# An adaLN transformer block: which round of the attention loop computes the projections of the next head pair

## The chip, the cores and the metric

The kernel runs on one core of one Trainium2 chip. The metric is device time in microseconds (us) from launch to end. Five engines run their own instruction streams and wait for each other through semaphores: PE (TensorE, matmuls), ACT (ScalarE), DVE (VectorE), POOL (GpSimd) and SP (SyncE, which here only issues DMAs). A matmul writes PSUM, which has eight banks of 128 x 512 f32; ACT and DVE read it from there.

## What is computed

Two adaLN blocks over four batches of 1024 tokens with 256 channels. The change touches only the first block's causal attention with 16 heads of 64, and the modulation vectors that are worked out beside it in the first batch:

```python
mod = (silu(L0_c) @ L0_wmod).reshape(4, 6, 1, -1)      # and the same for block 1
h = layernorm(x) * (1 + ca) + sa
latent_kv = h @ w_kv_down
k, v = split(latent_kv @ w_kv_up)                      # 16 heads of 64
q = h @ w_q
att = softmax(where(causal, q @ k.T * 64 ** -0.5, -inf))
x = x + ga * ((att @ v) @ w_out)
```

After it come a low-rank FFN, a second block with linear attention and MLP, and a mixture of experts; none of that is changed.

## The kernel before

Batch after batch goes through all stages. In the attention of a batch the heads go in `PAIRS` = 8 pairs, and each pair in three rounds (`ROUND_TILES` = (0, 2, 1, 5), (3, 7), (4, 6)): a round takes query tiles of 128 rows whose causal parts add up to 12 blocks of 128 keys, so each round has the same matmul work in scores and in values. There are `ROUNDS` = 24 rounds. Round m is the first of its pair when m is a multiple of 3; "a third round" is one with m = 2, 5, 8 and so on.

One round goes through the engines like this:

- PE `scores(m)` (L666) fills the score banks. It may start once DVE has taken the minima of round m-1.
- DVE `minimum` (L794) adds the mask, keeps the masked scores in SBUF and takes row minima, one call for a tile and a head. ACT `exponential` (L917) follows each. Once the last of a head is there, DVE `shuffle` (L801) transposes 32 x 32 blocks. After a third round come the reciprocals of the row sums, and `store_inverse` and `spread_inverse` send them through DRAM into `inverse_wide`.
- POOL `keep` (L865, seven copies) and SP `MOVES` (L1007, nine DMAs) bring the shuffled blocks into `placed`.
- PE `values(m)` (L688) multiplies `placed` by `v_t`. It stands two rounds later in PE's stream, behind `scores(m + 2)`. ACT `read_values` (L925) copies the result from `out_bank` into `yT`, and POOL `norm` (L875) scales it, four rounds after.

The projections of a pair are six jobs, `JOBS` = q0, q1, k0, k1, v0, v1, halves of the query, key and value projections (PE L710, L714, L720; ACT copies L901, L903, L905). `round_of` says in which round a pair's jobs stand. From round 2 on all jobs write one bank, `job_bank`, so each must wait until ACT has copied the one before. The first job of a round stands ahead of `values(m - 2)` on PE, the second behind it; `jobs_ahead` names the first. On ACT the copy of the first stands among the last exponentials of the round, that of the second behind `read_values`.

Into the first batch's rounds the modulation is fitted. `mod_products` (round 1), `mod_columns`, `mod_take` and `mod_values` (round 2) work it out. `mod_turn` (PE L756) transposes it into `out_bank`, `mod_rows_copy` (ACT L947) copies it out, and the next `values` may write `out_bank` only after that.

In the last rounds there are no jobs left. `output_part` (PE L730) starts the output projection of tiles 0 and 1 from the pairs that are scaled already, as filler, and behind the loop `head_output` (L1134) does the same for other tiles. The first work that needs the last pair is L1118: it waits for `norm` of round 21, and that for the last spread of the reciprocals.

Engines run their streams in the order in which the code is written; nothing is reordered by a scheduler. Before the change:

```python
def round_of(pair, j):
    return ROUNDS_OF * (pair - 1) + (JOBS.index(j) // 2 if (pair, j) != (1, "v0") else 1)
```

So pair 3, for one, had q0 and q1 in round 6, k0 and k1 in round 7, v0 and v1 in round 8. PE's stream of a round was:

```python
scores(m)
ahead = jobs_of(m) if m < FILLING else jobs_ahead(m)
for j in ahead:
    job(*j)
if m > 1:
    values(m - 2)
for j in jobs_of(m)[len(ahead):]:
    job(*j)
```

## Time and profile before

| | us |
|---|---|
| median of 3 runs | 1703.29 |
| the runs | 1703.29, 1702.17, 1703.40 |
| profiled execution, own time | 1701.55 |
| its span | 1700.1 |
| PE busy in the span | 1655.3 |
| DVE busy | 1225.7 |
| POOL busy | 868.3 |
| ACT busy | 846.6 |

The times of the rows are from the start of the span. The profiled execution is 1.74 us under the median of the three runs, and 1.45 us of it lie outside the span. The attention rounds of the four batches begin near 25, 450, 868 and 1285 us, and each takes about 205 us.

### The profile page before, as it was taken

To read this page: it belongs to the slowest core of one execution; us is meant where nothing else is said; L and a number is where in the kernel's file an instruction comes from. 1 tells how busy PE (TensorE), PEld (TensorE's weight loads), DVE (VectorE), ACT (ScalarE), POOL (GpSimd) and SP (SyncE) were. 2 spreads that over 40 slices of the span, in tenths; PEclk is the share of its full clock that TensorE was granted. 3 is DMA by queue.
4 is the path that set the end of the run, shared out by engine and by line. 5 is a ranking of instruction groups with operands and counts; after the bars stand their busy time and mean duration, and the time that the engine had idled before them with its cause. 6 is when DMAs were issued, how large, how long until landed. Compare 5 with 4: busy or idle time off the path is not lost.

```text
span 1700.1 us, 41069 instructions
## 1 busy us (share of the span) xinstructions
PE 1655.3 (97%) x16550; PEld 1133.1 (67%) x16550; DVE 1225.7 (72%) x2674; ACT 846.6 (50%) x1872; POOL 868.3 (51%) x1127
## 2 busy tenths in 40 slices
PE   9999999999999999999999999999999999999997
PEld 5566685768566667576856667756784666766666
DVE  5898957636699994762779997675468999677445
ACT  5667634233577762422457775432246776443232
POOL 3788853142188884222228888324114888731420
PEclk9999999999999999999999999999999999999999
DMA  6466572141565665032356655405045666620504
GB/s 193 121 157 152 140 180 94 29 72 44 160 153 137 151 144 170 1 63 38 89 136 157 149 144 135 149 2 96 5 118 133 148 152 144 157 106 2 100 0 126
DMA packets 143853, 189.11 MB, mean 111 GB/s; under 512 B 34512, under 2 KB 107696, under 8 KB 142640
## 3 DMA queue, kind: packets, MB, share of 16 engines
q1 hardware_dynamic: 125472, 179.14, 43.0%
q10 hardware_dynamic: 18192, 7.35, 1.8%
q8 instruction: 131, 2.15, 0.6%
q14 instruction: 58, 0.48, 0.1%
HBM read 88.32 MB, written 13.16 MB: 60 GB/s over the span
## 4 chain that ended last, share of the span: by engine, by line
PE 76%; DVE 13%; ACT 5%; POOL 2%; issue 2%; DMA 1%; SPq 1%; ACTq 0%; DVEq 0%; POOLq 0%
PE scores L470 13%; PE scores L666 11%; PE bank L688 11%; PE bank L470 5%; PE bank L710 4%; PE bank L714 3%; ACT prob L917 3%; PE bank L720 2%; DVE prob L801 2%; PE scores L1785 2%; PE scores L1725 2%; DVE hx L801 2%; PE scores L441 2%; PE scores L1134 2%; ACT hx L917 1%
## 5 line engine op out<-in xcount | busy, mean ns | idle before, releaser
L865 POOL COPY placed<-prob 32x768 f32<-32x768 f32 x448 | 368.0, 821 | 207.6 <-DVE prob L801 165.6
L301 POOL TENSOR_TENSOR rstd<-rstd,minus_half 128x2 f32<-128x2 f32 (+1 forms) x100 | 71.9, 721 | 486.7 <-DVE rstd L300 484.6
L688 PEld LDWEIGHTS bank<-placed,v_t 128*64 128x64 f32 x4608 | 255.0, 137 | 39.6 <-issue 39.4
L666 PE MATMUL scores<-k_t,q_t 64*128 64x512 f32 (+3 forms) x1536 | 274.0, 496 | 3.0 <-DVE neg_max L794 3.0
L688 PE MATMUL bank<-placed,v_t 128*64 128x128 f32 x4608 | 269.4, 273 | 1.9 <-DMA placed<-prob 1.7
L801 DVE STREAM_TRANSPOSE prob<-prob 128x1536 f32<-128x1536 f32 x128 | 220.0, 1757 | 37.0 <-ACT prob L917 37.0
L794 DVE CUSTOM_DVE_ANT_0 mod_rows<-scores,hx 128x128 f32<-128x128 f32 (+7 forms) x256 | 190.9, 746 | 37.6 <-PE scores L666 37.2
L666 PEld LDWEIGHTS scores<-k_t,q_t 64*128 64x128 f32 x1536 | 130.4, 187 | 116.6 <-issue 95.0
L865 POOL COPY placed<-hx 32x768 f32<-32x768 f32 x224 | 184.1, 822 | 30.5 <-DVE hx L801 13.5
L917 ACT ACTIVATE prob<-mod_rows,neg_max 128x128 f32<-128x128 f32 (+2 forms) x192 | 137.3, 715 | 118.8 <-DVE neg_max L794 115.9
L794 DVE CUSTOM_DVE_ANT_0 x<-scores,hx 128x128 f32<-128x128 f32 (+7 forms) x256 | 192.7, 753 | 0.0
L917 ACT ACTIVATE prob<-x,neg_max 128x128 f32<-128x128 f32 (+2 forms) x192 | 136.2, 709 | 0.0
L801 DVE STREAM_TRANSPOSE hx<-hx 128x1536 f32<-128x1536 f32 x64 | 112.0, 1750 | 6.2 <-ACT hx L917 6.2
L710 PE MATMUL bank<-hT,w_ring 128*64 128x512 f32 x448 | 108.2, 607 | 2.8 <-ACT q_t L901 2.8
L875 POOL TENSOR_TENSOR yT<-yT,inverse_wide 128x256 f32<-128x256 f32 (+2 forms) x128 | 91.7, 730 | 26.4 <-DMA inverse_wide<-inverse_scratch 19.4
L917 ACT ACTIVATE hx<-mod_rows,neg_max 128x640 f32<-128x640 f32 x64 | 59.9, 936 | 75.1 <-DVE neg_max L794 75.1
L1062 DVE TENSOR_TENSOR tmp<-bank,mod_rows 128x256 f32<-128x256 f32 x28 | 11.8, 423 | 115.0 <-PE bank L1118 70.0
L470 PE MATMUL scores<-mT,w 128*128 128x512 f32 x192 | 85.0, 592 | 0.0
L720 PEld LDWEIGHTS bank<-w_ring,latT 128*64 128x64 f32 x1024 | 55.1, 136 | 30.3 <-issue 18.2
L925 ACT COPY yT<-bank 128x256 f32<-128x256 f32 (+2 forms) x128 | 43.1, 362 | 60.5 <-PE bank L688 60.4
L720 PE MATMUL bank<-w_ring,latT 128*64 128x128 f32 x1024 | 68.6, 277 | 2.7 <-ACT k_t L903 2.7
L710 PEld LDWEIGHTS bank<-hT,w_ring 128*64 128x64 f32 x448 | 28.9, 137 | 59.5 <-issue 56.1
(253 smaller groups left out, 3107.3 us busy)
## 6 DMA issues: line engine op xcount, KB each, us to landing
placed<-prob SPq DMA_DIRECT2D x576, 96.0 KB, 2.6
f<-in_L_ffn_f SPq DMA_DIRECT2D x16, 2048.0 KB, 13.8
placed<-hx SPq DMA_DIRECT2D x288, 96.0 KB, 2.2
inverse_wide<-inverse_scratch SPq DMA_DIRECT2D x64, 256.0 KB, 4.3
slots_scratch<-high_rows SPq DMA_DIRECT2D x16, 512.0 KB, 6.6
inter<-slots_scratch SPq DMA_DIRECT2D x32, 256.0 KB, 4.7
mod_rows<-mod_scratch SPq DMA_DIRECT2D x32, 128.0 KB, 4.8
out<-x SPq DMA_DIRECT2D x16, 256.0 KB, 2.1
```

The costliest lines, as they stand in the source:

```text
L301: step = pool.do(lambda e, ts=ts: nc.gpsimd.tensor_tensor(rstd[:, ts], rstd[:, ts], minus_half[:, ts], op=ALU.pow), var, filled)
L470: step = pe.do(lambda e, n=n, w=w, m=m: nc.tensor.matmul(ps, w, m, start=n == 0, stop=n == len(pieces) - 1), copy, *after)
L666: last = nc.tensor.matmul(score_tiles[head][:, at_ // 512, at_ % 512:at_ % 512 + hi - lo], q_t[buf][rows_, tile * P:(tile + 1) * P], k_t[b ...
L688: last = nc.tensor.matmul(out_bank[rows_, at_:at_ + P], v_t[pair % 2][:, j, rows_], placed[m % 2][:, :, head, first_block(m, i) + j, :], s ...
L710: last = nc.tensor.matmul(ps[side, :], ring[:, c * P + side.start:c * P + side.stop], hT[:, c, cols], start=c == 0, stop=c == C - 1)
L714: last = nc.tensor.matmul(ps[side, :], ring[:, 2 * P + side.start:2 * P + side.stop], latT[:, cols], start=True, stop=True)
L720: last = nc.tensor.matmul(ps[side, t * P:(t + 1) * P], latT[:, at_ + side.start:at_ + side.stop], ring[:, 3 * P:4 * P], start=True, stop=True)
L794: nc.vector.tensor_tensor_reduce(masked_scores[head][:, cols], score_tiles[head][:, :, :].rearrange("p a n -> p (a n)")[:, cols], future[: ...
L801: nc.vector.transpose(p_, p_).then_inc(flow["shuffled"], 1)
L865: nc.gpsimd.tensor_copy(placed[m % 2][target * GROUP:(target + 1) * GROUP, source, :, :, :], prob[m % 3][source * GROUP:(source + 1) * GRO ...
L875: last = nc.gpsimd.tensor_tensor(dst, dst, out_place(m, lo, hi, inverse_wide), op=ALU.mult)
L917: nc.scalar.activation(prob[m % 3][:, :, head, blocks_in(m, i), :], masked_scores[head][:, columns_in(m, i)].rearrange("p (n g i) -> p g n ...
```

## The change

From the third pair on (`pair` 2 and up, counted from 0) every job moves by one place: q0 goes one round earlier, behind its `values`; q1 and k0 share the next round, then k1 and v0, then v1 with q0 of the following pair. The places themselves, one ahead of `values` and one behind, stay. In the first batch's round 2 both jobs stand behind `values(0)`. ACT copies the first job of round 3 (first batch) or of round 2 (other batches) ahead of all exponentials of that round. `mod_turn` and `mod_rows_copy` go from the end of round 3 into round 4: the turn behind `scores(4)`, the copy behind the first two exponentials. `output_part(0)` goes from round 22 to round 21.

```diff
         def jobs_of(m):
             pair = m // ROUNDS_OF + 1
-            return [(pair, j) for j in JOBS if round_of(pair, j) == m] if pair < PAIRS else []
+            return [(p, j) for p in (pair, pair + 1) if p < PAIRS for j in JOBS if round_of(p, j) == m]
 
         def round_of(pair, j):
-            return ROUNDS_OF * (pair - 1) + (JOBS.index(j) // 2 if (pair, j) != (1, "v0") else 1)
+            if pair < 2:
+                return ROUNDS_OF * (pair - 1) + (JOBS.index(j) // 2 if (pair, j) != (1, "v0") else 1)
+            return ROUNDS_OF * (pair - 1) + (JOBS.index(j) - 1) // 2
...
-        MOD_ROUND = 3
+        MOD_ROUND = 4
...
-                if b == 0 and m == MOD_ROUND - 1:
+                if b == 0 and m == MOD_ROUND - 2:
                     e.wait_ge(flow["mod_rows_ready"], 1)
...
             def mod_turn():
-                e.wait_ge(flow["values_read"], MOD_ROUND - 1)
+                e.wait_ge(flow["values_read"], MOD_ROUND - 2)
...
+                if b == 0 and m == MOD_ROUND:
+                    mod_turn()
                 ahead = jobs_of(m) if m < FILLING else jobs_ahead(m)
                 for j in ahead:
                     job(*j)
+                if m == ROUNDS - 3:
+                    output_part(0)
                 if m == ROUNDS - 1:
                     output_part(1)
-                if m == ROUNDS - 2:
-                    output_part(0)
                 if m > 1:
                     values(m - 2)
                 for j in jobs_of(m)[len(ahead):]:
                     job(*j)
-                if b == 0 and m == MOD_ROUND:
-                    mod_turn()
...
+                if m == 2 and b or m == 3 and b == 0:
+                    for j in ahead:
+                        job(*j)
                 for i in range(large):
                     for head in range(HEADS):
                         exponential(m, i, head)
+                    if b == 0 and i == 0 and m == MOD_ROUND:
+                        mod_rows_copy()
...
                 early = m == 1 or len(tiles_in(m)) > 2
+                if m == 2 or m == 3 and b == 0:
+                    early = None
                 for j in ahead if early else ():
                     job(*j)
                 exponential(m, large, 0)
-                for j in ahead if not early else ():
+                for j in ahead if early is False else ():
                     job(*j)
...
-                if b == 0 and m == MOD_ROUND:
-                    mod_rows_copy()
```

PE's stream in the first batch, from `values(0)` in round 2 to `scores(4)`, before (L688 values, L720 v1 of pair 1, L666 scores, L710 q jobs, L756 the modulation's turn):

```order
L688 MATMUL bank<-placed_64,v_t_59 64x128 x24
L720 MATMUL bank<-w_ring_55,latT 64x128 x8
L666 MATMUL scores<-k_t_60,q_t_53 128x128 x2
L666 MATMUL scores<-k_t_60,q_t_53 128x384 x2
L666 MATMUL scores<-k_t_60,q_t_53 128x256 x4
L666 MATMUL scores<-k_t_60,q_t_53 128x512 x2
L710 MATMUL bank<-hT,w_ring_54 64x512 x4
L688 MATMUL bank<-placed_65,v_t_59 64x128 x24
L710 MATMUL bank<-hT,w_ring_54 64x512 x4
L756 MATMUL bank<-ident,mod_cols 96x128
L666 MATMUL scores<-k_t_60,q_t_53 128x512 x6
```

The same stretch now (all lines after the diff's first are two higher):

```order
L690 MATMUL bank<-placed_64,v_t_59 64x128 x24
L722 MATMUL bank<-w_ring_55,latT 64x128 x8
L712 MATMUL bank<-hT,w_ring_54 64x512 x4
L668 MATMUL scores<-k_t_60,q_t_53 128x128 x2
L668 MATMUL scores<-k_t_60,q_t_53 128x384 x2
L668 MATMUL scores<-k_t_60,q_t_53 128x256 x4
L668 MATMUL scores<-k_t_60,q_t_53 128x512 x2
L712 MATMUL bank<-hT,w_ring_54 64x512 x4
L690 MATMUL bank<-placed_65,v_t_59 64x128 x24
L716 MATMUL bank<-latT,w_ring_54 64x512 x2
L668 MATMUL scores<-k_t_60,q_t_53 128x512 x6
L758 MATMUL bank<-ident,mod_cols 96x128
```

The query job q0 of pair 2 went ahead of `scores(3)`, k0 stands where q1 stood, and the turn went behind `scores(4)`.

ACT's stream in the first batch, from `read_values(0)` through round 3, before (L925 `read_values`, L905 and L901 copies of jobs, L917 exponentials, L947 the copy of the turn):

```order
L925 COPY yT<-bank 128x128
L905 COPY v_t_61<-bank 128x512
L917 ACTIVATE prob_62,row_sum<-mod_rows,neg_max 128x4x32
L917 ACTIVATE prob_62,row_sum<-x,neg_max 128x4x32
...
L901 ACTIVATE q_t_52<-bank 128x512
L917 ACTIVATE prob_62,row_sum<-mod_rows,neg_max 128x4x192
L917 ACTIVATE prob_62,row_sum<-x,neg_max 128x4x192
L925 COPY yT<-bank 128x2x128
L901 ACTIVATE q_t_52<-bank 128x512
L947 COPY tmp<-bank 96x128
```

And now:

```order
L907 COPY v_t_61<-bank 128x512
L903 ACTIVATE q_t_52<-bank 128x512 x2
L919 ACTIVATE prob_62,row_sum<-mod_rows,neg_max 128x4x32
L919 ACTIVATE prob_62,row_sum<-x,neg_max 128x4x32
...
L919 ACTIVATE prob_62,row_sum<-mod_rows,neg_max 128x4x192
L919 ACTIVATE prob_62,row_sum<-x,neg_max 128x4x192
L927 COPY yT<-bank 128x2x128
L905 COPY k_t_58<-bank 128x512
```

Both query copies of pair 2 now stand ahead of the first exponential of round 3.

PE's stream in the last rounds of a batch, from the end of round 20 to `scores(23)`, before (L730 is `output_part`):

```order
L720 MATMUL bank<-w_ring_55,latT 64x128 x8
L688 MATMUL bank<-placed_64,v_t_59 64x128 x24
L720 MATMUL bank<-w_ring_55,latT 64x128 x8
...
L666 MATMUL scores<-k_t_60,q_t_53 128x512 x2
L688 MATMUL bank<-placed_65,v_t_59 64x128 x24
L666 MATMUL scores<-k_t_60,q_t_53 128x512 x6
L730 MATMUL bank<-wout,yT 128x256 x6
L688 MATMUL bank<-placed_64,v_t_59 64x128 x24
```

And now, with the v0 job of the last pair already ahead of `scores(20)`:

```order
L722 MATMUL bank<-w_ring_55,latT 64x128 x8
L690 MATMUL bank<-placed_64,v_t_59 64x128 x24
...
L668 MATMUL scores<-k_t_60,q_t_53 128x512 x2
L732 MATMUL bank<-wout,yT 128x256 x6
L690 MATMUL bank<-placed_65,v_t_59 64x128 x24
L668 MATMUL scores<-k_t_60,q_t_53 128x512 x6
L690 MATMUL bank<-placed_64,v_t_59 64x128 x24
```

Round 20 has one job fewer, and the filler moved from behind `scores(22)` to behind `scores(21)`.

## Rows read from the trace of the kernel before

**Rows 1.** The page, section 1: busy us (share), instructions.

```profile
PE 1655.3 (97%) x16550; PEld 1133.1 (67%) x16550; DVE 1225.7 (72%) x2674; ACT 846.6 (50%) x1872; POOL 868.3 (51%) x1127
```

**Rows 2.** PE's timeline, first batch, rounds 2 to 5: start us, us, group [idle <-releaser].

```profile
43.57 2.84 PE L688 MATMUL bank<-placed,v_t 128*64 128x128 f32 x48
46.24 1.04 PE L720 MATMUL bank<-w_ring,latT 128*64 128x128 f32 x16
47.83 2.86 PE L666 MATMUL scores<-k_t,q_t 64*128 64x128 f32 x20 [0.55 <-DVE neg_max L794]
50.62 1.94 PE L710 MATMUL bank<-hT,w_ring 128*64 128x512 f32 x8
52.39 2.79 PE L688 MATMUL bank<-placed,v_t 128*64 128x128 f32 x48
57.78 3.58 PE L710 MATMUL bank<-hT,w_ring 128*64 128x512 f32 x8 [2.60 <-ACT q_t L901]
...
68.80 2.86 PE L666 MATMUL scores<-k_t,q_t 64*128 64x512 f32 x16
```

**Rows 3.** One stretch of it: us, PE busy (x), granted clock, DMA share, GB/s.

```profile
57.70:61.30 3.60, 3.52 (x9) 0.53 0.69 174
```

**Rows 4.** ACT's timeline, first batch, rounds 2 to 4.

```profile
49.29 0.59 ACT L905 COPY v_t<-bank 128x512 f32<-128x512 f32 x1
53.67 0.40 ACT L917 ACTIVATE prob<-mod_rows,neg_max 128x128 f32<-128x128 f32 x1 [3.79 <-DVE neg_max L794]
...
59.47 0.35 ACT L925 COPY yT<-bank 128x256 f32<-128x256 f32 x1
...
61.89 0.25 ACT L947 COPY tmp<-bank 96x128 f32<-96x128 f32 x1
...
63.51 0.72 ACT L917 ACTIVATE prob<-mod_rows,neg_max 128x512 f32<-128x512 f32 x1 [1.37 <-DVE neg_max L794]
```

**Rows 5.** DVE's timeline, first batch, shuffles of round 3 and first minimum of round 4.

```profile
58.67 3.44 DVE L801 STREAM_TRANSPOSE prob<-prob 128x1536 f32<-128x1536 f32 x2 [1.51 <-ACT prob L917]
...
62.70 0.69 DVE L794 CUSTOM_DVE_ANT_0 mod_rows<-scores,hx 128x512 f32<-128x512 f32 x1 [0.59 <-PE scores L666]
```

**Rows 6.** PE's timeline, second batch, rounds 3 and 4.

```profile
470.49 2.86 PE L666 MATMUL scores<-k_t,q_t 64*128 64x128 f32 x20 [0.58 <-DVE neg_max L794]
...
478.07 1.94 PE L710 MATMUL bank<-hT,w_ring 128*64 128x512 f32 x8 [0.23 <-ACT q_t L901]
...
486.56 1.08 PE L714 MATMUL bank<-latT,w_ring 128*64 128x512 f32 x4
```

**Rows 7.** ACT's timeline, second batch, round 4: the copy of the round's first job.

```profile
485.94 0.56 ACT L903 COPY k_t<-bank 128x512 f32<-128x512 f32 x1
```

**Rows 8.** PE's timeline, end of the attention: first batch, then second batch.

```profile
187.62 2.86 PE L666 MATMUL scores<-k_t,q_t 64*128 64x512 f32 x16
...
233.16 1.99 PE L1118 MATMUL bank<-wout,yT 128*128 128x256 f32 x8 [0.48 <-POOL yT L875]
...
650.76 1.99 PE L1118 MATMUL bank<-wout,yT 128*128 128x256 f32 x8
```

**Rows 9.** DVE's timeline, first batch: first minimum of round 21.

```profile
197.00 0.25 DVE L794 CUSTOM_DVE_ANT_0 mod_rows<-scores,hx 128x128 f32<-128x128 f32 x1
```

**Rows 10.** POOL's timeline, end of the attention: first batch (three), second batch.

```profile
195.48 1.42 POOL L875 TENSOR_TENSOR yT<-yT,inverse_wide 128x256 f32<-128x256 f32 x2
...
204.95 6.12 POOL L865 COPY placed<-prob 32x768 f32<-32x768 f32 x7 [1.77 <-issue]
...
649.12 2.10 POOL L875 TENSOR_TENSOR yT<-yT,inverse_wide 128x384 f32<-128x384 f32 x3 [4.67 <-DMA inverse_wide<-inverse_scratch]
```

**Rows 11.** PE's timeline, first batch, rounds 17 and 18, steady state.

```profile
167.72 2.84 PE L688 MATMUL bank<-placed,v_t 128*64 128x128 f32 x48 [0.16 <-DMA placed<-prob]
...
174.15 1.94 PE L710 MATMUL bank<-hT,w_ring 128*64 128x512 f32 x8
```

**Rows 12.** ACT's timeline, first batch, round 18: the copy of its first job.

```profile
176.62 0.58 ACT L901 ACTIVATE q_t<-bank 128x512 f32<-128x512 f32 x1
```

## The prediction

> **What bounds the kernel now.** I read the page's busy times first. PE is busy for 1655.3 of 1700.1 us [rows 1], and the change removes no matmul and adds none. All it can win is idle time of PE and time at the lower clock; all it can lose is new idle time. So I went through PE's timeline for gaps in the four attention stages. In the steady rounds there are next to none. They lie in three places.
>
> First, the first batch's rounds 2 and 3: 0.55 us before `scores(3)`, which waits for DVE's minima, and 2.60 us before q1 of pair 2, which waits until ACT has copied q0 out of the shared job bank [rows 2]. Behind that gap the granted clock is 0.53 on average for 3.6 us, so for nearly all of it PE ran at 1.2 in place of 2.4 GHz [rows 3]; q1 took 3.58 us where q0, the same eight matmuls, took 1.94 [rows 2], 1.7 us lost. Second, the same place in the second batch: 0.58 and 0.23 us, and a little at k1 of round 4, which starts at 486.56, straight after ACT's copy of k0 ends at 485.94 + 0.56 [rows 6, 7]. Third, the end of each attention stage.
>
> The end has to be read on all engines. The first minimum of round 21 starts at 197.00, 9.4 us after `scores(20)` at 187.62 [rows 8, 9]. From there DVE works through rounds 21 to 23 almost without pause, POOL through `keep(21)` at 204.95 and all that follows to `norm` at 231.69, and PE waits 0.48 us for that `norm` before L1118 at 233.16 [rows 8, 10]. So L1118 stands 233.16 - 187.62 = 45.5 us behind the start of `scores(20)`, by DVE, POOL and DMA, and PE fills its time with `values` and the output filler. In the second batch `norm(21)` is done at 649.12 + 1.4 (two of the three operations in 2.10) = 650.5, and L1118 starts at 650.76: PE and that chain arrive within 0.2 us of each other [rows 8, 10]. Two things therefore count: how much PE has to do before `scores(20)`, and not how much after.
>
> **First batch, rounds 2 to 5.** Lengths from start to start: scores 50.62 - 47.83 = 2.8, a q job 1.8, `values` 2.7, a k or v job 1.0 [rows 2]; the turn I put at 0.3.
> - Nothing differs up to v1 of pair 1, which ends at 46.24 + 1.04 = 47.3. The next instruction on PE is now q0 of pair 2. It writes the bank that v1 wrote, and ACT copies v1 only at 49.29 to 49.88, because round 2's exponentials and `read_values(0)` stand ahead of it [rows 2, 4]. Before, `scores(3)` lay in that time. Now PE idles from 47.3 to 49.9: 2.6 us, as long as the wait that the change removes.
> - q0 to 51.7, `scores(3)` to 54.5, q1 to 56.3 (q0 has been copied by then), `values(1)` to 59.0, k0 to 60.0, `scores(4)` to 62.8, the turn to 63.1, k1 to 64.1.
> - ACT now has q1's copy ahead of round 3's exponentials. They began at 53.67 [rows 4]; now the copy waits for q1, and they begin at 57.0. They ran until 59.47, 5.8 us with one 0.6 us copy among them [rows 4], so now to 62.2. The first shuffle of round 3 came 58.67 - 53.67 = 5.0 us behind the first exponential, 4.5 without the copy [rows 4, 5]: now 61.2 to 61.5, and both are done 3.4 us later, at 64.7 to 64.9.
> - Only then can DVE take round 4's first minimum, and 63.51 - 62.70 = 0.8 us later comes its exponential [rows 4, 5]; two of 0.72 and the copy of the turn, 0.25 [rows 4], end at about 67.2. `values(2)` waits for that copy, since the turn lies in its bank. PE idles from 64.1 to 67.3, 3.2 us. Before, the turn and its copy lay in front of `scores(4)` and nobody waited.
> - `values(2)` to 70.0 and v0 to 71.0: `scores(5)` starts at 71.0, against 68.80 [rows 2]. That is 2.2 us later, with v0 already done. From here PE paces the rounds again, and every third round's `scores` has the same work between it and the next one as before. `scores(20)`, and with it L1118, comes 2.2 us later. The v0 job done early helps nothing: it belongs to the stretch in which PE has time.
>
> A rule of the Trainium skill bears on the third point. PSUM — Partial Sum Buffer, section "Engine vs sequencer instructions", says that ScalarE's queue is strictly first in, first out. By that rule no exponential of round 3 passes the waiting copy, and this stretch gives +2.2; could they pass it, they would begin at 53.67 as before, the second idle time would be gone, and the stretch would give about -1. No row here shows ready work behind a waiting copy.
>
> **The clock.** The one wait of 2.60 us in the attention was followed by 3.4 us or so at 1.2 GHz, a loss of 1.7 us [rows 2, 3], which 68.80 contains. The change puts two waits of 2.6 and 3.2 us in its place. The 0.55 us before `scores(3)` [rows 2] was not followed by one. One case does not say that each such wait brings one, so I give each somewhat over a half: no drop, one, or two cost 0, 1.7 or 3.4 us on top. PE has work right behind both waits, so a drop delays `scores(5)` in full. One is likeliest.
>
> **The other batches.** q0 of pair 2 fills the 0.58 us before `scores(3)`, and ACT's early copy of v1 costs nothing, since ACT waits for minima there. The 0.23 us before the q1 job [rows 6] goes as well: that place is now k0's, and q1 stands ahead of `values(1)`, so it has been copied by then. That and the wait at k1 make 0.95 us. But v0, 1.0 us, now stands ahead of `scores(5)`, and v0 must wait for ACT's copy of k1, which DVE's pace holds at 486.5: `scores(5)` is unmoved, and so is `scores(20)`. At the end PE gets to L1118 about 1 us early and waits for `norm`; 650.76 becomes 650.55 [rows 8, 10]. I take -0.2 for each of three batches, -0.5 with rounding for a worse fourth.
>
> **The filler.** `output_part(0)` goes behind `scores(21)`, which now ends at 187.62 + 2.8 + 1.0 + 2.7 + 2.8 = 196.9. It needs the `norm` that ends at 195.48 + 1.42 = 196.9 [rows 8, 10], so it waits 0.1 at most; the wait for minima before `scores(22)` is filled. Both fall into PE's spare time: 0.
>
> **Steady rounds.** The first round of a pair now starts 0.8 us later against DVE, because q0 (1.8) stands where v1 (1.0) stood. Its first job ended at 174.15 + 1.94 = 176.09, and ACT copied it at 176.62, with 0.5 us to spare [rows 11, 12]. Now ACT waits up to 0.3 us, and the last exponentials, shuffles and DMAs of that round go with it. `values` of such a round already waited 0.16 us for a DMA in one pair [rows 11]. The bounds are 0 and 0.3 us for each of 24 pairs, 0 to 7. Most pairs show no such wait and have spare time there, so I take 0.03 each, 0.7 in all.
>
> **The sum.** 2.2 - 0.5 + 0.7 = 2.4 us without a clock drop, 4.1 with one, 5.8 with two. On the profiled execution's 1701.55 that is 1705.7 for one drop. The median of the runs lies 1.74 higher; from its 1703.29 I get 1707.4, or 1705.7 and 1709.1.
>
> **The rivals.**
> - PE sets the end (faster). If DVE and POOL had room in rounds 21 to 23, the gain of each gap would last: in the first batch 0.55 + 2.60 + 1.7 + 0.48, in the second about 1, less in the others, some 7 us, 1696. It needs the first batch's q0 not to wait for v1's copy as well, by which ACT would have to be 2.6 us earlier. Against it speak 49.29 [rows 4] and the unbroken chain [rows 8 to 10].
> - The delay is absorbed (no change). DVE catches up in the steady rounds, where it sometimes waits for scores, so that L1118 comes as before. With no or one drop this gives 1703 to 1705. Against it: DVE's waits in a third round are for PE's `scores`, so it cannot get ahead of them.
> - The steady rounds lose (slower still). If ACT's wait for q1 of 0.3 us goes through in most pairs, 24 x 0.25 = 6 replaces 0.7: 1712.5. It decides from the point at which the DMAs of a pair's first round land after PE is ready.
>
> **How the numbers follow.** The forecast holds 0.70: no drop 0.18, one 0.32, two 0.20. PE sets the end 0.08, absorbed 0.14, steady rounds 0.08. A measurement of this kernel can tell 0.2%, 3.4 us. Below 1699.9 only the first rival lies: faster 0.08. Within: the absorbed case, most of no drop and a quarter of one drop, 0.38. Slower 0.54. The range from 1702.5 to 1711.5 takes in 0, one and two drops, the absorbed case and half of the last rival.
>
> **What would show it.** PE idle 2.6 us before the L712 job at 49.9 in the first batch, ACT's first exponential of round 3 at 57, 3 us of idle before `values(2)`, `scores(5)` at 71 or 1.7 later for each stretch at 1.2 GHz; in the second batch `scores(5)` within 0.1 us of its old place against the batch's start, and a wait for `norm` of some 0.7 us before L1125 (L1118 before). If q0 of pair 2 starts at 47.3, or `values(2)` does not wait, the first batch's part is wrong; if L1125 does not wait longer for POOL than before, the reading of the end is.

## The result and the profile after

The changed kernel takes 1712.18 us (median of 4 runs, 1710.45 to 1713.53), the kernel before, run beside it, 1703.35 (4 runs, 1702.17 to 1704.61). The ratio is 1.0055, with a 95% interval of 1.0043 to 1.0068: slower, by some 9 us. The forecast was 1707.4, with a range that ended at 1711.5. The sign was right; the time lies outside the range.

The profiled execution took 1710.45 us, 4.75 above the 1705.7 that the sum gave for it. Its page has the same work as in [rows 1]. First come the span, then busy time, share and number of instructions of each engine.

```profile
span 1709.1 us, 41069 instructions
PE 1658.8 (97%) x16550; PEld 1138.3 (67%) x16550; DVE 1227.0 (72%) x2674; ACT 853.4 (50%) x1872; POOL 866.8 (51%) x1127
```

The span is 9.0 us longer, and PE is busy for only 3.5 us more. To place the rest I cut each batch's attention at three starts on PE's timeline: the first matmul of `scores(0)`, `scores(5)` and `scores(20)`, and that of L1125 (L1118 before). The lengths in us:

| | scores(0) to (5) | (5) to (20) | (20) to L1125 | all | change |
|---|---|---|---|---|---|
| first batch, before | 43.34 | 118.82 | 45.54 | 207.70 | |
| after | 48.37 | 118.74 | 45.49 | 212.60 | +4.90 |
| second, before | 37.20 | 118.19 | 45.00 | 200.39 | |
| after | 38.24 | 118.43 | 45.20 | 201.87 | +1.48 |
| third, before | 37.21 | 117.97 | 45.00 | 200.18 | |
| after | 37.21 | 118.45 | 44.91 | 200.57 | +0.39 |
| fourth, before | 37.38 | 118.51 | 44.99 | 200.88 | |
| after | 37.84 | 119.10 | 45.99 | 202.93 | +2.05 |

That is 8.8 of the 9.0 us: 4.9 in the first batch, where the sum had 3.9 (2.2 and one stretch at 1.2 GHz), and 3.9 in the other three, where it had next to nothing.

Two of these numbers are partly luck. In the first batch of the kernel before, `scores(5)` to `scores(20)` holds some 0.85 us of small waits; of the four other executions with the same code there, three have 117.97 or 117.98 us and one 118.99. So 4.90 may be too small for what the change costs in the first batch. And 1.04 of the 1.48 us in the second batch lie ahead of `scores(5)`, where PE waited once for a DMA:

```profile
473.60 2.84 PE L690 MATMUL bank<-placed,v_t 128*64 128x128 f32 x48 [1.50 <-DMA placed<-prob]
```

In the ten other executions with the new order in that batch (the experiments below), `scores(0)` to `scores(5)` took 37.21 to 37.35 us there, against 37.20 before.

**The first batch.** PE's timeline, rounds 2 to 5, to be read against [rows 2]. Columns: start, duration, engine and line, operation with its tiles, number of matmuls, and in brackets the idle time before them and what ended it.

```profile
46.24 1.05 PE L722 MATMUL bank<-w_ring,latT 128*64 128x128 f32 x16
49.98 2.48 PE L712 MATMUL bank<-hT,w_ring 128*64 128x512 f32 x8 [2.68 <-issue]
52.38 3.96 PE L668 MATMUL scores<-k_t,q_t 64*128 64x128 f32 x20
...
64.64 1.08 PE L716 MATMUL bank<-latT,w_ring 128*64 128x512 f32 x4
68.75 4.27 PE L690 MATMUL bank<-placed,v_t 128*64 128x128 f32 x48 [3.04 <-issue]
72.84 1.05 PE L722 MATMUL bank<-w_ring,latT 128*64 128x128 f32 x16
73.83 2.43 PE L668 MATMUL scores<-k_t,q_t 64*128 64x512 f32 x14
```

Both waits are there. PE idles 2.68 us before q0 of pair 2 and 3.04 us before `values(2)`. Behind the first, `scores(3)` takes 3.96 us in place of 2.8, around the end of the second `values(2)` takes 4.27 in place of 2.7. These are two stretches at 1.2 GHz. In two windows laid on them the granted clock (the number behind the five engines' busy times) is 0.52 and 0.53:

```profile
51.10:54.60 3.50, 3.50 (x14) 1.61 (x12) 2.28 (x9) 0.60 (x1) 2.87 (x4) 0.52 0.40 96
68.20:71.80 3.60, 3.05 (x30) 3.08 (x32) 3.43 (x6) 3.31 (x8) 3.35 (x5) 0.53 0.67 162
```

In windows of a quarter of a microsecond each stretch is 3.41 us long, as was the one in [rows 3]. The first begins at 51.2, 1.3 us after the wait has ended, the second at 68.3, while PE still waits.

Why the second wait is there shows in DVE's timeline and then ACT's, round 3. DVE has the first minimum of the round at 54.8. Its exponential starts at 58.75, behind q1's copy, which had waited 5.17 us for the q job on PE.

```profile
54.49 0.29 DVE L796 CUSTOM_DVE_ANT_0 mod_rows<-scores,hx 128x128 f32<-128x128 f32 x1 [1.15 <-PE scores L668]
```

```profile
58.26 0.60 ACT L903 ACTIVATE q_t<-bank 128x512 f32<-128x512 f32 x1 [5.17 <-PE bank L712]
...
58.75 0.39 ACT L919 ACTIVATE prob<-mod_rows,neg_max 128x128 f32<-128x128 f32 x1
...
68.41 0.24 ACT L949 COPY tmp<-bank 96x128 f32<-96x128 f32 x1
```

So ready work stood 4 us behind a waiting copy, and the turn's copy came at 68.41, 0.3 us before `values(2)`.

**The steady rounds.** PE's timeline in the second batch, from `scores(11)` on:

```profile
564.56 2.85 PE L668 MATMUL scores<-k_t,q_t 64*128 64x512 f32 x16
567.34 1.09 PE L722 MATMUL bank<-w_ring,latT 128*64 128x128 f32 x16
568.27 2.79 PE L690 MATMUL bank<-placed,v_t 128*64 128x128 f32 x48
570.96 1.94 PE L712 MATMUL bank<-hT,w_ring 128*64 128x512 f32 x8
572.83 2.43 PE L668 MATMUL scores<-k_t,q_t 64*128 64x128 f32 x18
```

No wait is printed, and yet a pair now takes 23.68 or 23.69 us in every pair of these three batches that has no wait for a DMA, against 23.59 or 23.60 before. From `values` to q0 it is 570.96 - 568.27 = 2.69 us. In the kernel before the same `values` had a v job behind it, 2.62 us from start to start. ACT's timeline shows the copy that q0 needs, v0's:

```profile
570.25 0.56 ACT L907 COPY v_t<-bank 128x512 f32<-128x512 f32 x1
```

It ends at 570.81, just before q0. Whether q0 really waits for it is tried in v0_early below. At five pairs from `scores(5)` to `scores(20)` this makes 0.45 us a batch.

**The end of a batch.** PE waits for `norm` longer, as [rows 8] let one expect; the fourth batch is the worst. PE's timeline, then POOL's: `norm` itself waits for the DMA that spreads the inverse.

```profile
1495.03 1.99 PE L1125 MATMUL bank<-wout,yT 128*128 128x256 f32 x8 [1.45 <-POOL yT L877]
```

```profile
1493.57 2.77 POOL L877 TENSOR_TENSOR yT<-yT,inverse_wide 128x384 f32<-128x384 f32 x4 [5.86 <-DMA inverse_wide<-inverse_scratch]
```

### The profile page after: what moved, and what is told of

Read it like the earlier page. It is cut to its first block, busy times and chain, and to the rows that moved or that the text cites. A ratio compares the mean times of both kernels' runs of the same rounds, so it can differ in the third digit from the quotient of the medians.

```text
span 1709.1 us, 41069 instructions
## 1 busy us (share of the span) xinstructions
PE 1658.8 (97%) x16550; PEld 1138.3 (67%) x16550; DVE 1227.0 (72%) x2674; ACT 853.4 (50%) x1872; POOL 866.8 (51%) x1127
## 4 chain that ended last, share of the span: by engine, by line
PE 74%; DVE 10%; POOL 6%; ACT 4%; issue 3%; DMA 2%; SPq 2%; POOLq 0%; ACTq 0%; DVEq 0%
PE scores L470 13%; PE scores L668 11%; PE bank L690 10%; PE bank L470 5%; PE bank L712 5%; POOL placed L867 4%; PE bank L716 3%; PE bank L722 3%; ACT prob L919 2%; DVE prob L803 2%; PE scores L1792 2%; PE scores L441 2%; PE scores L1732 2%; PE scores L1371 1%; PE scores L1375 1%
```

## The experiments

The numbers of all runs stand first, in one table. "First" and "later" are from `scores(0)` to L1125 (or the line that answers to it), in the first batch and summed over the other three; "stretches" is the time at 1.2 GHz between 44 and 76 us. Ratios are to the kernel before on the same chip.

| run | scores(0) to (5), first | first | later | stretches | ratio | interval |
|---|---|---|---|---|---|---|
| before | 43.34 | 207.70 | 601.45 | 3.4 | | |
| after | 48.37 | 212.60 | 605.37 | 6.8 | 1.0055 | 1.0043 to 1.0068 |
| after_again | 49.80 | 215.21 | 604.69 | 10.2 | 1.0045 | 1.0029 to 1.0061 |
| first_only | 49.82 | 213.71 | 602.17 | 10.2 | 1.0041 | 1.0027 to 1.0055 |
| later_only | 43.36 | 206.55 | 605.12 | 3.4 | 1.0022 | 1.0012 to 1.0031 |
| filler_only | 43.34 | 206.38 | 601.52 | 3.4 | 1.0006 | 0.9997 to 1.0016 |
| early_copy | 41.33 | 205.00 | 601.74 | 0 | 0.9995 | 0.9986 to 1.0004 |
| copy_ahead | 44.68 | 210.42 | 605.19 | 3.4 | 1.0041 | 1.0028 to 1.0054 |
| v1_mid | 46.57 | 210.52 | 603.83 | 6.8 | 1.0044 | 1.0031 to 1.0057 |
| both_fixed | 43.57 | 209.53 | 604.14 | 3.4 | 1.0023 | 1.0015 to 1.0032 |
| late_q | 42.16 | 205.03 | 603.11 | 0 | 1.0015 | 1.0006 to 1.0024 |
| all_fixed | 41.65 | 206.85 | 604.62 | 0 | 1.0013 | 1.0004 to 1.0023 |
| v0_early | 42.04 | 206.15 | 602.86 | 0 | 1.0013 | 1.0005 to 1.0022 |
| early_two | 40.39 | 205.17 | 601.84 | 0 | 0.9991 | 0.9982 to 1.0000 |
| full_fixed | 41.67 | 207.12 | 602.50 | 0 | 1.0014 | 1.0005 to 1.0022 |
| full_fixed2 | 41.66 | 206.65 | 603.73 | 0 | 1.0013 | 1.0004 to 1.0022 |

In the kernels of the experiments the lines lie 1 to 4 below those of the changed kernel. `MOVED_JOBS` in their edits says whether the jobs stand in the new order.

### The change taken apart by batch and part

first_only has the new order, the early copy and the moved turn in the first batch alone; later_only has the new order in the other three, and the filler; filler_only has the filler alone.

```diff
+        MOVED_JOBS = b == 0        # first_only
+        MOVED_JOBS = b > 0         # later_only
+        MOVED_JOBS = False         # filler_only
...
-            if pair < 2:
+            if pair < 2 or not MOVED_JOBS:
...
-                if m == 2 and b or m == 3 and b == 0:
+                if (m == 2 and b or m == 3 and b == 0) and MOVED_JOBS:
...
-                if m == ROUNDS - 3:
+                if m == ROUNDS - 2:        # first_only
                     output_part(0)
```

> The new job order, the early query copy and the later turn in the first batch alone; the other batches and the filler as before the change. Theory 1 (the loss of 5.0 us between scores(0) and scores(5) of the first batch is the two new waits and the two stretches at 1.2 GHz, and it is carried to the end): 4.9 us slower than before, scores(5) of the first batch at 73 to 74 us, the other batches' attention as long as before within 0.3 us each. Rival (the first batch's loss is caught up later, the loss comes from the later batches): within 1 us of before.

> The new job order in batches 2 to 4 and the filler in round 21; the first batch's jobs, copies and turn as before. Theory 1a (the later batches' 3.9 us come from the order itself: a job more ahead of scores(20), and ACT waiting for q1): 3.5 to 4 us slower, with scores(5) to scores(20) longer by 0.2 to 0.6 us in each of these batches. Theory 1b (as predicted, the order costs next to nothing there; the 3.9 us were DMAs that landed late by chance): 0 to 1 us slower, and the wait of 1.5 us before values(0) in the second batch is gone or stands elsewhere.

> Only output_part(0) goes from round 22 to round 21, in all batches. As predicted: no difference beyond 0.3 us, since both places lie in PE's spare time between scores(20) and L1118. Rival (the filler ahead of values(19) delays the reads and the norms behind it, and with them the end of the attention): 0.3 to 1 us later in each batch, 1 to 4 us in all, seen in a longer way from scores(20) to the first full output product.

The first batch alone costs 7.0 us, with the same two waits (2.67 and 3.04) and three stretches' worth of 1.2 GHz at them. That is 2 us more than the theory had, since the theory took over the 4.9 us and the two stretches of one execution. `scores(5)` came at 75.34, past the 73 to 74 expected, by the third stretch. The other batches cost 3.7, and their pairs take 23.68 to 23.69 us as in the changed kernel. The filler costs nothing that can be told. The parts add up to 10.7 us by their ratios, against 9.4 and 7.7 in the two measurements of the whole, within the intervals.

### The changed kernel once more

> The changed kernel once more, without an edit, for a second execution to read beside the first and for its time on the chip of the next three kernels. My theory, that the stretches at 1.2 GHz behind a wait of 2 to 3 us come in most executions and not in all: the two waits in the first batch are there again within 0.15 us (2.5 to 2.7 before q0 of pair 2, 3.0 before values(2)), the number of stretches behind them may be another one (none to three of 3.4 us), and scores(5) - scores(0) is 45.0 us plus 1.7 us for each. Rival, that code and waits alone decide: the same two stretches, 48.4. Time 1.0045 to 1.0065 of the kernel before.

The waits were 2.69 and 3.04 us. The stretches were 3.4 and, in one piece at the second wait, 6.8 us. The same code and the same waits thus do not give the same time at 1.2 GHz. The six runs spread from 1705.32 us, at a granted clock of 0.999, to 1713.51, at 0.995.

### The old order with the copies ahead

early_copy leaves the jobs and the filler on PE where they were before; the turn alone stands behind `scores(4)`, as in the changed kernel. In the first batch ACT copies q0 of pair 2 ahead of round 3's exponentials and the turn ahead of round 4's.

```diff
+        MOVED_JOBS = False
...
-                if m == 2 and b or m == 3 and b == 0:
+                if m == 2 and b and MOVED_JOBS or m == 3 and b == 0:
                     for j in ahead:
                         job(*j)
+                if b == 0 and m == MOD_ROUND:
+                    mod_rows_copy()
                 for i in range(large):
...
-                    if b == 0 and i == 0 and m == MOD_ROUND:
-                        mod_rows_copy()
```

> The order of before in all batches, with two things changed in the first batch: ACT copies q0 of pair 2 ahead of round 3's exponentials, and the modulation's turn stands behind scores(4) with its copy ahead of all exponentials of round 4. Theory 1 (in the first batch PE waits for ACT's place in the order, and pays a stretch at 1.2 GHz on top): the waits of 2.6 us and of 3 us are both gone, no stretch at 1.2 GHz in the attention, scores(5) at about 65.4 in place of 68.8, 3 to 3.5 us faster than before. Rival (DVE or the moved blocks set scores(5) anyway): scores(5) no earlier than 67.5 and within 1.5 us of before.

The 2.60 us wait of the kernel before is gone, and with it the stretch. But k1 of pair 2 now waits 1.84 us for ACT's copy of k0, and `scores(5)` is only 2.0 us earlier. The time does not differ measurably, where 3 to 3.5 us were expected. The rival had that time, but its reason, DVE or the moved blocks, shows only as a new wait of 0.33 us for DVE before `scores(4)`. early_two moves k0's copy ahead too:

```diff
-                if m == 2 and b and MOVED_JOBS or m == 3 and b == 0:
+                if m == 2 and b and MOVED_JOBS or m in (3, 4) and b == 0:
```

> The kernel before with the order of PE as it was and three copies of ScalarE moved in the first batch: q0 of pair 2 ahead of round 3's exponentials and the turn's copy ahead of round 4's (as in the run of the early copies), and now k0 of pair 2 ahead of round 4's exponentials too, for which k1 waited 1.84 us there. My theory: this wait goes, scores(5) starts 39.5 to 40.5 us behind scores(0) in place of 41.33 and 43.34, S20 - S5 and the end stay, the time is 1.0 to 1.8 us below that of the early copies and 2.5 to 4 us below the kernel before. Rival, that DVE's minima hold up scores(5) from there: 41.0 or later, nothing more is won.

`scores(5)` came at 40.39, as expected, and the time fell to 0.9991 of the kernel before, 1.5 us where 2.5 to 4 were expected, with 1.0000 as the end of the interval. It is the fastest version of this study and hardly more than equal. Of the 3 us won up to `scores(5)` the rounds after it gave some back: `scores(5)` to `scores(20)` took 119.16 us, where 117.97 is the length without a wait. In the first of these rounds PE waits 0.37 us for ACT's copy of v0, and this first pair takes 24.46 us in place of 23.59; in the new order it is 0.7 to 1.2 us longer than the others in all_fixed, full_fixed and full_fixed2, where `scores(5)` comes early too. PE's timeline shows the wait that is left before `values(2)`:

```profile
60.21 1.08 PE L717 MATMUL bank<-latT,w_ring 128*64 128x512 f32 x4
62.18 2.84 PE L691 MATMUL bank<-placed,v_t 128*64 128x128 f32 x48 [0.89 <-ACT k_t L906]
64.82 1.06 PE L717 MATMUL bank<-latT,w_ring 128*64 128x512 f32 x4
65.81 2.86 PE L669 MATMUL scores<-k_t,q_t 64*128 64x512 f32 x16
```

### The changed kernel with one wait mended

copy_ahead puts the turn's copy ahead of round 4's exponentials:

```diff
+                if b == 0 and m == MOD_ROUND:
+                    mod_rows_copy()
                 for i in range(large):
...
-                    if b == 0 and i == 0 and m == MOD_ROUND:
-                        mod_rows_copy()
```

> The changed kernel with ScalarE's copy of the modulation turn put ahead of round 4's exponentials instead of behind its first tile; nothing else differs. My theory, that the first batch lost its time in two waits and in the two stretches at 1.2 GHz behind them: the wait of 3.04 us before values(2) goes, and with it the stretch at 1.2 GHz in which values(2) took 4.27 us in place of 2.7. The first wait (2.5 to 2.7 us before q0 of pair 2) stays, with its stretch. scores(5) starts 45.5 or less behind scores(0) in place of 48.37, more likely 44.0 (3.0 of wait and 1.4 to 1.6 of clock), so the time is 3.0 to 4.6 us below that of the changed kernel, 3.7 to 5.5 above that of the kernel before. Rival, that the DVE work of round 4 paces this place anyway: the wait moves to scores(5), which stays at 47 to 48, and the time falls by under 1.5 us.

The 3.04 us before `values(2)` are gone, and a wait of 2.09 us stands one job later: v0 needs ACT's copy of k1, which lies behind the same exponentials. PE's timeline:

```profile
65.02 2.79 PE L691 MATMUL bank<-placed,v_t 128*64 128x128 f32 x48
69.90 1.41 PE L723 MATMUL bank<-w_ring,latT 128*64 128x128 f32 x16 [2.09 <-ACT k_t L906]
71.24 4.17 PE L669 MATMUL scores<-k_t,q_t 64*128 64x512 f32 x16
```

The stretch at 1.2 GHz came behind this wait. It now hits `scores(5)`, so that `scores(5)` starts early (44.68) and the stage behind it is 120.94 us long. The first wait, again 2.70 us, had no stretch behind it. The edit acts only in round 4 and so is not the reason; the granted clock stayed at 1.00:

```profile
48.00:54.00 6.00, 3.30 (x26) 1.51 (x24) 5.74 (x12) 3.58 (x8) 4.20 (x6) 1.00 0.45 109
```

The time hardly followed: 1.0041, some 7 us above the kernel before, where 3.7 to 5.5 were expected. Against the changed kernel, 9.4 and 7.7 above it, nothing is won that is clear of the intervals.

v1_mid puts the copy of v1 of pair 1 ahead of round 2's last exponential in the first batch:

```diff
+                middle = jobs[:1] if b == 0 and m == 2 else []
+                for j in middle:
+                    job(*j)
                 exponential(m, large, 1)
                 if m > 1:
                     read_values(m - 2)
-                for j in jobs[len(ahead):]:
+                for j in jobs[len(ahead) + len(middle):]:
```

> The changed kernel with ScalarE's copy of v1 of pair 1 put ahead of the last exponential of round 2 in the first batch (it stood behind that exponential and read_values(0)); nothing else differs. My theory: the wait before q0 of pair 2 shrinks from 2.5-2.7 us to about 1.0, no stretch at 1.2 GHz follows it (0.55 us of idle was not followed by one, 2.6 was), and everything up to scores(5) comes 3.0 to 3.5 us earlier, 1.6 by the wait and 1.7 by the clock; the second wait before values(2) stays at about 3 us with its own stretch. scores(5) - scores(0) 44.9 to 45.4 in place of 48.37; time 3 us below that of the changed kernel. Rival, that the stretch at 1.2 GHz comes with any idle time of this order: only 1.6 us are won, 46.7. Second rival, that the copy in the middle delays DVE's shuffles and so round 3's start: under 1 us is won.

The first wait fell to 1.13 us, and no stretch followed. The second wait stayed at 3.15 us, with 6.8 us at 1.2 GHz from 1.3 us before its end on, so `scores(5)` came at 46.57 and not at 44.9 to 45.4. The part of the wait was right; the clock at the other one was not. The time, 1.0044, is not 3 us below the changed kernel's either, but within its intervals.

both_fixed has both edits.

> Both of the edits together: the turn's copy ahead of round 4's exponentials, and v1's copy ahead of the last exponential of round 2 in the first batch. My theory, that the two waits and their stretches are all that the first batch lost: scores(5) comes 41.0 to 42.5 us behind scores(0), below the 43.34 of the kernel before, with no stretch at 1.2 GHz after 50 us. What is left against the kernel before is the loss of the later batches (3.9 us in the profiled executions) less 1 to 2 us: time 1 to 3 us above that of the kernel before. Rival, that the first batch is then paced by DVE and ACT and not by PE: scores(5) at 43 to 44, time 3 to 5 us above the kernel before.

Waits of 1.11 and, before v0, 2.21 us, one stretch, and 1.0023: 3.9 us above the kernel before, where the changed kernel was 9.4 and 7.7 above it. `scores(5)` came at 43.57, where the rival had put it. What held it was ACT's late copy of k1, as in copy_ahead, and no wait for DVE. all_fixed moves that one as well:

```diff
-                if (m == 2 and b or m == 3 and b == 0) and MOVED_JOBS:
+                if (m == 2 and b or m in (3, 4) and b == 0) and MOVED_JOBS:
```

> The new order with three copies moved on ScalarE in the first batch: the two of the run before (v1 ahead of round 2's last exponential, the turn's ahead of round 4's exponentials) and that of k1 of pair 2, now also ahead of round 4's exponentials, so that v0 behind values(2) finds its bank free. There the run before waited 2.2 us and a stretch at 1.2 GHz followed. My theory, that this wait was the rest of what the first batch loses by the new order: no idle time over 1.2 us and no stretch at 1.2 GHz from 44 us on, scores(5) 40.6 to 42.0 us behind scores(0) in place of 43.57, the time 1.5 to 3.5 us below that of the run with two copies moved, 0.5 to 2.5 us above the kernel before. Rival, that DVE's minima then hold up scores(5): a wait for DVE takes the place, scores(5) at 43 or later, and nothing is won.

`scores(5)` at 41.65, no stretch, the largest wait 1.13 us, 1.0013. The first batch takes 206.85 us: 5.8 less than in the changed kernel's first execution and 8.4 less than in its second, by three copies on ACT alone. Against early_two, the old order with its copies mended, 1.3 us are left up to `scores(5)` (41.65 to 40.39). That is about the v0 job of 1.0 us that the new order puts ahead of `scores(5)`; no run takes that job away to show it.

### The steady rounds

late_q is later_only with q1's copy between the last two exponentials of a pair's first round. v0_early then also puts v0's copy ahead of the last two exponentials of a pair's third round.

```diff
-                early = m == 1 or len(tiles_in(m)) > 2
+                early = m == 1 or len(tiles_in(m)) > 2 and not (MOVED_JOBS and m > 3)       # late_q
...
+                early = m == 1 or len(tiles_in(m)) > 2 and not (MOVED_JOBS and m > 3) or MOVED_JOBS and m > 3 and m % 3 == 2      # v0_early
```

> Batches two to four in the new order as in the run of the later batches alone, but in the first round of a pair ScalarE copies q1 between the two exponentials of the last tile, no longer ahead of both; the first batch is as before. Two readings of the steady rounds (23.68 us a pair in place of 23.60, with no wait shown) are told apart. By the first, the prediction's own, ScalarE's wait for q1 holds up the exponentials and so the round: the wait of 0.2 us goes, a pair takes 23.60 again, and S20 - S5 of the batches falls by 0.4 to 0.5 each, 1.2 to 1.5 us in all, to 2.3 us above the kernel before. By the second, the 0.07 to 0.09 us is lost on PE itself at the place where q0 now follows values and not scores: a pair stays at 23.68, and the time stays 3 to 4 us above the kernel before.

> As the run with q1's copy between the exponentials (batches two to four in the new order, the first as before), and in the third round of a pair ScalarE copies v0 ahead of the last two exponentials in place of between them, 1.2 us earlier. It tells where the 0.09 to 0.10 us that a pair lost come from. My theory: q0 behind values waits for this copy (values to q0 2.69 us from start to start, where the same seven places without a wait show 2.62); the 0.07 us go and a pair takes 23.61 to 23.63 us; S20 - S5 falls from 118.43 to 118.0 or 118.1. Rival, that the hand-over from v to q and from q to scores costs this on PE itself: 23.68 to 23.69 as before. Second rival, that the last exponentials and their shuffles are then 0.5 us late and values of the next round but one waits for a DMA: a pair over 23.7.

In late_q the pairs stayed at 23.68 and 23.69: the wait of ACT for q1, which the prediction had named, is not what lengthens them. The time, 2.6 us above the kernel before, lay between the two readings. In v0_early they fell to 23.56, below the kernel before, and `values` to q0 is 2.62 us: it was q0 that waited for v0's copy. Its timeline, PE:

```profile
561.55 2.79 PE L691 MATMUL bank<-placed,v_t 128*64 128x128 f32 x48
564.17 1.89 PE L713 MATMUL bank<-hT,w_ring 128*64 128x512 f32 x8
565.98 2.86 PE L669 MATMUL scores<-k_t,q_t 64*128 64x128 f32 x20
```

But the time did not follow (1.0013 to 1.0015). What PE won up to `scores(20)` it lost behind it: in the second batch the two stages are 118.43 and 44.84 us in late_q, 118.02 and 45.38 in v0_early. DVE's timeline of full_fixed, third batch, shows where it went: the shuffle behind the last exponentials of round 20 waits 0.62 us for ACT, because v0's copy now stands ahead of them, and the first minimum of round 21 follows at 1033.87. PE's L1129 comes 35.8 us later.

```profile
1030.31 1.78 DVE L804 STREAM_TRANSPOSE hx<-hx 128x1536 f32<-128x1536 f32 x1 [0.62 <-ACT hx L920]
...
1033.87 0.25 DVE L797 CUSTOM_DVE_ANT_0 mod_rows<-scores,hx 128x128 f32<-128x128 f32 x1
```

```profile
1069.69 1.99 PE L1129 MATMUL bank<-wout,yT 128*128 128x256 f32 x8 [1.02 <-POOL yT L878]
```

In the changed kernel, same batch, the same shuffle waits 0.19 us, and the minimum is at 1039.38, 35.5 us ahead of L1125:

```profile
1035.82 1.78 DVE L803 STREAM_TRANSPOSE hx<-hx 128x1536 f32<-128x1536 f32 x1 [0.19 <-ACT hx L919]
...
1039.38 0.25 DVE L796 CUSTOM_DVE_ANT_0 mod_rows<-scores,hx 128x128 f32<-128x128 f32 x1
```

```profile
1074.91 1.99 PE L1125 MATMUL bank<-wout,yT 128*128 128x256 f32 x8 [0.70 <-POOL yT L877]
```

In the kernel before it is 1032.53 and 1068.14, 35.6 us. Behind `scores(0)` the minimum comes at 164.57 us (before), 165.04 (after) and 164.85 (full_fixed). The end of the batch goes with DVE's rhythm, and that one loses 0.3 to 0.5 us by the new order in both placements of ACT's copies that were tried. In each later batch of v0_early, and in all batches of full_fixed and full_fixed2, the last spread of the inverse is issued 39.7 to 39.8 us behind `scores(20)`, and 39.3 to 39.4 in all others.

### Everything mended at once

full_fixed is all_fixed with the two steady copies as well: the new order in all batches, five copies moved. full_fixed2 is the same with the filler back in round 22.

```diff
-                early = m == 1 or len(tiles_in(m)) > 2
+                early = m == 1 or len(tiles_in(m)) > 2 and m < 5 or m > 4 and m % 3 == 2
...
-                if m == ROUNDS - 3:
+                if m == ROUNDS - 2:        # full_fixed2 only
                     output_part(0)
```

> The new order of PE in all four batches with every ScalarE copy that was found late moved: in the first batch v1's, the turn's and k1's, and in the steady rounds of all batches q1's (between the last two exponentials) and v0's (ahead of them). My theory, that the new order costs only by these copies: first batch 206 to 207.5 us from scores(0) to L1125 with no stretch at 1.2 GHz after 44 us, each later batch 200.2 to 201.2, a pair 23.6 us or less; the time is from 1.0 us below to 1.5 above the kernel before, ratio 0.9995 to 1.001. Rival, that the order has a price of its own, at the end of a batch or in its first rounds, that no copy mends: 2 to 4 us above the kernel before, and the trace shows in which stage.

> The same with output_part(0) back in round 22, where it stood in the kernel before. My theory, that the filler's place is worth nothing (its own run gave 1.0006, with zero inside the interval): the same time as its neighbour within 0.7 us, and L1125 as far behind scores(20). Rival, that the filler in round 21 holds up scores(22) by its 0.4 us wait for norm, and with it the end of each batch: 0.4 us a batch, 1.6 us faster than its neighbour.

The first batch and the pairs came out as in the theory, the time nearer to the rival: both stay 2.2 to 2.4 us above the kernel before, with intervals from 0.7 to 3.7. The order keeps a price in every placement of the copies that was tried; whether another one removes it is not shown. By the table it is some 1.8 us in the first batch (207.12 and 206.65 against 205.00 and 205.17 of the old order with its copies moved) and 0.1 to 0.8 us in each later one (602.50 and 603.73 against 601.45 to 602.17). The filler's place is worth nothing, which its own run had said too.

## Why the prediction was wrong in size, and right in its mechanism in the first batch alone

The profiled execution lies 4.75 us above the sum: 0.8 in the first batch (4.9 against 2.2 + 1.7 and a fourth of the 0.7), 3.9 in the other three, for which the sum had -0.5 and the rest of the 0.7, so nothing. That the first batch looks nearly right is partly luck. The three executions with both waits (after, after_again, first_only) took 213.8 us there on average, the five with the code of before (before, later_only, filler_only, late_q, v0_early) 206.4. That is 7.5 us more, by first_only's ratio 7.0, and not 4.1.

- **The two waits of the first batch: right.** It had 2.6 us before q0 and 3.2 before `values(2)`; measured were 2.68 and 3.04. It had q0 from 49.9 on and got 49.98. Its rule, that ready exponentials do not pass q1's waiting copy, showed in the trace: the minimum of 54.5 to 54.8 waited for its exponential until 58.75. That agrees with what the Trainium skill says in PSUM — Partial Sum Buffer, section "Engine vs sequencer instructions", that ScalarE's queue is strictly first in, first out. Mending ACT's copies one after the other took the waits away, and with them most of what the first batch had lost.
- **The clock: the term that failed first.** "One is likeliest" was the choice; two came. With two the prediction's own `scores(5)` is 71.0 + 3.4 = 74.4, and 73.83 was measured, so the path without the clock was sized some 0.4 us too long (0.2 us are the part of the second stretch that fell into the wait), and the number of stretches was wrong. In the three executions that had both waits, each wait had at least one stretch at it, and twice the second had one of double length: 2.7 stretches on average, 2.8 us more than the one that was taken. The choice rested on one row of the kernel before. By the executions since then, waits of 2.60 to 2.85 us were followed by one in 6 of 9 executions (the kernel before, later_only and filler_only with one, late_q and v0_early without; after, after_again and first_only with one, copy_ahead without), which is the "somewhat over a half" that was taken, but waits of 3.04 to 3.15 us in 4 of 4, three times at double length. The two were priced alike; so few executions cannot tell the chances apart, but in these rounds the double length came at the longer waits alone.
- **"Steady rounds ... 0.03 each": the step that failed most in the other batches.** Over 24 pairs 0.09 makes 2.2 us, and the sum had 0.7. Its bounds (0 to 0.3 a pair) held the truth, 0.09; the value taken did not, and neither did its place: not ACT waiting for q1, with late DMAs behind it (late_q took that wait away, and the pairs stayed), but PE's q0 waiting for ACT's copy of v0. The prediction had looked only at whether the moved job's copy is late, and not at whether the job finds its bank free on time. In the kernel before the copy ended 541.01 - 534.76 = 6.25 us behind its `scores`, after 570.81 - 564.56 = 6.25; v1 came 0.08 us behind it, q0 0.15. A place without slack was there to see. v0_early shows the part that is ACT's copy: with it 1.1 us earlier (ending 5.17 us behind `scores`) the pairs are at 23.56.
- **"-0.2 for each of three batches": wrong sign.** The later batches lost 3.9 us in the first execution and 3.0 on average (604.7 us over seven executions with the changed kernel's order and copies there, 601.7 over five with the old ones). Of these 3.0 us, 0.5 lie ahead of `scores(5)`, 1.7 between `scores(5)` and `scores(20)`, and 0.7 behind it. `scores(5)` did stay where it was in the third batch (37.21), and L1125 waits for `norm` 0.70 us there, both as written. But `scores(20)` does not: it comes 0.48 us later. And the argument that PE then has spare time until `norm` fails because DVE, which sets `norm`, is fed by the same rounds and is late with them.
- **The fourth batch**: the prediction left it to rounding. It is the worst, +2.05 here and 201.3 to 203.6 us in all eleven executions with a new order there, against 200.5 to 201.4 with the old one. Its end waits for the DMA of the inverse (5.86 us of idle on POOL, against 4.67 in the same batch of the kernel before, as in that of [rows 10]).
- **The filler at nothing: right** by two runs. It waits 0.43 us for `norm` and not 0.1, and that costs nothing.
- **The rivals.** "PE sets the end" needed a first batch without waits; the opposite came. "Absorbed": the stage from `scores(5)` to `scores(20)` took 118.74 us, where the old order without a wait takes 117.97; nothing was caught up. "Steady rounds lose" had 6 us by ACT's wait for q1, which late_q took away without a change in the pairs; its sign was that of the truth.

What stays open: why the fourth batch loses more than the second and third. The last spread of the inverse is issued 39.3 us behind `scores(20)` there, before and after alike, but took 4.4 to 5.8 us to land in the seven executions with the changed kernel's order and copies, and 4.0 to 4.6 in the five with the old ones. In the four with q1's copy moved (late_q, v0_early, full_fixed, full_fixed2) it took 4.1 to 4.4, and the batch 201.3 to 202.5 us against 202.0 to 203.6. So q1's copy may have a part in this batch after all; how, no run shows. Open is also why a second stretch at 1.2 GHz follows at once in some executions and not in others with the same waits.

## What to carry to other kernels

When a job is moved on the engine that paces a kernel, ask of every shared buffer both questions: is the moved job's reader late, and does the moved job find the reader of its predecessor done; a predecessor's copy that ends within 0.1 us of being needed has no slack to give. An in-order engine with copies among its exponentials should have each copy placed by hand for the new order, since moving the jobs without them cost 7 us in the first batch here and three moved copies took nearly all of it back. Mend the old order in the same way before the two are compared: with its own copies moved it stayed 1.7 us ahead in that batch. And where two engines stand within tenths of each other, a mended rhythm of the one shows up as idle time behind it: read the distance to the other's last step before counting a gain.

## What the runs showed of the hardware

Code and waits alone do not fix the clock. In the first batch's rounds 2 to 5, waits of 2.60 to 2.85 us of PE were followed by 3.4 us at 1.2 GHz in six of nine executions. In late_q and v0_early, whose first batch is that of the kernel before, PE waited 2.85 and 2.73 us for q0's copy, and the granted clock stayed at its full value; in the kernel before 2.60 us sufficed. At waits of 3.04 to 3.15 us there were 3.4 us once and 6.8 us in one piece three times, and the clock fell 0.4 to 1.3 us before the wait had ended. Waits of 2.09 and 2.21 us were each followed by 3.4 us, one of 1.84 us and those of 0.9 to 1.1 by none.

Elsewhere in the kernel it is no different. Before L1125 of the fourth batch (L1126 there) PE waited 1.98 us in copy_ahead, and 3.4 us at 1.2 GHz came at its end; in later_only it waited 2.38 us at the same place, and none came. Between 11.4 and 12.9 us, ahead of the attention, a stretch of 3.4 or 6.8 us begins in 8 of the 16 profiled executions, though no wait between 2 and 20 us is longer than 1.12 us. The code up to there is the same in all kernels. In these eight `scores(0)` starts at 26.25 to 27.13 us, in the others at 25.38 to 25.70; lengths counted from `scores(0)` leave that out. In v1_mid, at the wait of 3.15 us, PE did its 48 matmuls of `values(2)` in 5.39 us at a granted clock of 0.50, where 2.79 is usual:

```profile
67.40 5.39 PE L691 MATMUL bank<-placed,v_t 128*64 128x128 f32 x48 [3.15 <-issue]
```

```profile
66.20:72.80 6.60, 5.40 (x52) 5.43 (x53) 5.66 (x6) 3.96 (x10) 6.07 (x8) 0.50 0.56 133
```

The mean granted clock over all executions of a kernel goes with this in the main: 0.9950 in the changed kernel's first four and 0.9960 in its next six, 0.9960 and 0.9954 in first_only and v1_mid, 0.9970 to 0.9975 in the kernel before, 0.9978 and 0.9979 in both_fixed and all_fixed. The changed kernel's ten executions are 0.0014 to 0.0019 below the kernel before. Of 1700 us that is 2.4 to 3.2 us at the full clock, by estimate the price of 1.4 to 1.9 stretches, and about a third of what the change cost.
